# Turning the row maxima of a two-pass attention: DRAM transfer in place of a TensorE transposition

## The reference

```
x = x + cross_attention0(layernorm(x), ctx, mask)     # 6404 keys, padding mask
x = x + self_attention + mixture of experts           # 1024 keys
x = x + (causal self_attention, cross_attention1(x, ctx), feed-forward)
x = x + mixture of experts
# attention, per head:  softmax(q k^T / sqrt(8)) v,   softmax by exp(s - max(s))
```

## Time and profile before

| what | value |
|---|---|
| median of 3 runs | 2885.43 us (2884.71 to 2887.26) |
| the profiled execution's own time | 2884.41 us |
| its span, first to last instruction | 2882.7 us |
| TensorE busy | 2455.8 us, 85% |
| VectorE busy | 2370.1 us, 82% |
| ScalarE busy | 2154.9 us, 75% |
| GpSimd busy | 226.4 us, 8% |
| mean granted TensorE clock | 0.93 of full speed |

### The profile page before, as it was taken

One profiled execution on the slowest core, in us unless ns is written; L12 is line 12 of the kernel. 1 busy time (PEld: TensorE's weight loads), 2 busy tenths in 40 slices (PEclk: granted clock), 3 DMA queues, 4 the chain that ended last, 5 costly groups with the idle time before them and its releaser, 6 DMA issues.

```text
span 2882.7 us, 57521 instructions
## 1 busy us (share of the span) xinstructions
PE 2455.8 (85%) x22475; PEld 777.0 (27%) x22475; DVE 2370.1 (82%) x2782; ACT 2154.9 (75%) x4063; POOL 226.4 (8%) x556
## 2 busy tenths in 40 slices
PE   3499999999999994799459955999999999999955
PEld 2222222222222221222123312222222222222223
DVE  6699999999999983677337635999999999999824
ACT  3189999999999994466315641899999999999941
POOL 4001101010000001000000040000000010000000
PEclk8699999999999997899769966999999999999987
DMA  4211111101101100110111132011101111011000
GB/s 136 71 33 40 41 43 43 41 28 35 34 28 40 29 5 18 49 35 29 36 50 37 39 103 68 26 30 31 38 28 38 31 29 40 28 36 33 6 4 8
DMA packets 76606, 109.17 MB, mean 38 GB/s; under 512 B 17600, under 2 KB 56308, under 8 KB 76340
## 3 DMA queue, kind: packets, MB, share of 16 engines
q1 hardware_dynamic: 74548, 101.12, 12.0%
q0 software_dynamic: 1792, 4.37, 0.8%
HBM read 73.93 MB, written 22.42 MB: 33 GB/s over the span
## 4 chain that ended last, share of the span: by engine, by line
PE 67%; DVE 18%; ACT 6%; issue 4%; SPq 2%; DMA 2%; POOL 1%; ACTq 0%; POOLq 0%; DVEq 0%
PE ps L1280 66%; DVE maxima L1094 12%; ACT probs L884 3%; ACT probs L846 2%; DVE scratch L960 1%; SPq L448 1%; DVE maxima L1053 1%; ACT acc_out L827 1%; POOL probs L648 1%; DMA qa_stage<-q_cross 1%; DMA o_self<-acc_out 0%; PE ps L1288 0%; DVE stats L965 0%; DVE z L975 0%; DVE z L960 0%
## 5 line engine op out<-in xcount | busy, mean ns | idle before, releaser
L1094 DVE TENSOR_REDUCE maxima<-ps 128x1 f32<-128x920 f32 x1792 | 1889.9, 1111 | 102.0 <-PE ps L1280 102.0
L884 ACT ACTIVATE probs<-ps 128x512 f32<-128x512 f32 (+1 forms) x3264 | 1762.4, 594 | 146.3 <-PE ps L1280 146.1
L1280 PE MATMUL ps<-probs,v_stage 128*16 128x256 f32 (+1 forms) x13568 | 1150.0, 403 | 1.5 <-ACT probs L846 1.1
L1280 PE MATMUL ps<-k_stages,qa_stage 64*128 64x460 bf16 (+2 forms) x4032 | 801.5, 370 | 182.9 <-DMA qa_stage<-q_cross 67.3
L1280 PE MATMUL ps<-qb_stage,k_stages 64*128 64x512 bf16 (+4 forms) x3712 | 799.0, 381 | 42.3 <-ACT probs L846 17.6
L1280 PEld LDWEIGHTS ps<-k_stages,qa_stage 64*128 64x128 bf16 (+1 forms) x4032 | 209.5, 94 | 1023.8 <-issue 507.8
L1280 PEld LDWEIGHTS ps<-probs,v_stage 128*16 128x16 f32 x13568 | 234.8, 94 | 422.0 <-issue 364.5
L1053 DVE TENSOR_REDUCE maxima<-ps 128x1 f32<-128x1024 f32 (+7 forms) x256 | 246.8, 987 | 111.6 <-PE ps L1280 110.3
L846 ACT ACTIVATE probs<-ps 128x512 f32<-128x512 f32 (+1 forms) x448 | 229.4, 556 | 141.8 <-PE ps L1280 136.9
L1280 PEld LDWEIGHTS ps<-qb_stage,k_stages 64*128 64x128 bf16 (+1 forms) x3712 | 208.1, 93 | 343.6 <-ACT probs L846 99.9
L654 POOL COPY v_stage<-by_key 128x400 f32<-128x400 f32 (+1 forms) x96 | 40.5, 423 | 1376.0 <-PE ps L1280 1211.4
(11 more groups left out here) (212 smaller groups left out, 932.7 us busy)
## 6 DMA issues: line engine op xcount, KB each, us to landing
k_stages<-k_cross SPq DMA_DIRECT2D x64, 150.2 KB
k_stages<-k_cross SPq DMA_DIRECT2D x64, 150.0 KB
k_cross<-probs SPq DMA_DIRECT2D x24, 384.0 KB, 2.7
scratch<-acc_out SPq DMA_DIRECT2D x512, 16.0 KB
k_stages<-k_cross SPq DMA_DIRECT2D x64, 100.1 KB
k_stages<-k_cross SPq DMA_DIRECT2D x64, 100.0 KB
qa_stage<-q_cross SPq DMA_DIRECT2D x128, 48.0 KB
qb_stage<-q_cross SPq DMA_DIRECT2D x128, 48.0 KB, 4.8
```

The source lines that it names most:

```text
L884: return nc.scalar.activation(probs[0:m, probs_slot(a, j, i), :], ps[0:m, b_bank(a, use), :], ACT.Exp, scale=float(E) ** -0.5)
L1094: nc.vector.tensor_reduce(maxima[:, at, seg:seg + 1], ps[:, A_BANK + 2 * (g % 2):A_BANK + 2 * (g % 2) + 2, 0:a.segment], AX_XY, ALU.max).t ...
L1280: return nc.tensor.matmul(out_, lhsT, rhs, start=start, stop=stop)
```

## The change

In the long attentions the transposition, the copy and the use of the bank ring go. Instead put_maxima, on SyncE, waits for half_parts itself, writes it element by element (128 x 12 elements of 2 bytes) into a DRAM tensor laid out as 12 rows of 128, waits for that to land (`_max_out`), and then issues the two transfers into qb_stage from DRAM. GpSimd waits for `_max_out` before it overwrites half_parts. `ahead` goes from 28 + 12 to 28 + 14 units. Pass B waits for one semaphore fewer in each step.

```
-    a.ahead = len(a.max_units) + 12
+    a.ahead = len(a.max_units) + 14
-    a.turn_step = 20
-    a.turn_tile = a.step_tiles[a.turn_step + 1][0]
...
+                a.m_dram = dram("m_" + a.name, [2, 3, QT, P], BF16)
...
         def tile_use(a, j, i):
-            return 1 + j * (a.key_tiles + 1) + i + (i >= a.turn_tile and j + 1 < a.n)
+            return j * a.key_tiles + i
...
                 def put_maxima(j):
-                    sp.wait_ge(sem(a.name + "_max_rows"), j + 1)
+                    sp.wait_ge(sem(a.name + "_max_parts"), j + 1)
+                    sp.dma_start(a.m_dram[j % 2].rearrange("a t q -> q a t"), half_parts[:],
+                                 allow_slow_non_contiguous=True).then_inc(sem(a.name + "_max_out"), DMA)
+                    sp.wait_ge(sem(a.name + "_max_out"), (j + 1) * DMA)
                     for side in range(a.sides):
                         rows = qb_stage[side * SIDE + ROW_MAX:side * SIDE + ROW_MASK, j % a.ring, 0:BANK]
                         sp.dma_start(rows.rearrange("a (t q) -> a t q", t=QT),
-                                     max_rows[0:3 * QT, :]).then_inc(sem(a.name + "_max_in"), DMA)
+                                     a.m_dram[j % 2]).then_inc(sem(a.name + "_max_in"), DMA)
...
                     if j >= 1:
-                        pool.wait_ge(sem(a.name + "_scores"), turn_use(a, j - 1) + 1)
+                        pool.wait_ge(sem(a.name + "_max_out"), j * DMA)
...
-                        if i == a.turn_tile and j + 1 < a.n:
-                            copy_turned(j + 1)
...
                     free = tile_use(a, j, tiles[-1]) - a.b_banks + 1
                     if free >= 1:
-                        if probs_before(free):
-                            pe.wait_ge(sem(a.name + "_probs"), probs_before(free))
-                        pe.wait_ge(sem(a.name + "_max_rows"), turns_before(free))
+                        pe.wait_ge(sem(a.name + "_probs"), free)
...
-                        if t == a.turn_step and j + 1 < a.n:
-                            turn_maxima(j + 1)
```

More of the change, by code:

```diff
@@ L336, in transformer @@
             a.banks_before = sum(len(b.v_banks) for b in before)
+            if a.cross:
+                a.m_dram = dram("m_" + a.name, [2, 3, QT, P], BF16)
             a.k_dram = dram("k_" + a.name, [3, P, a.keys], BF16)
@@ L378, in tile_use @@
         def tile_use(a, j, i):
-            return 1 + j * (a.key_tiles + 1) + i + (i >= a.turn_tile and j + 1 < a.n)
-        def turn_use(a, j):
-            return 0 if j == 0 else 1 + (j - 1) * (a.key_tiles + 1) + a.turn_tile
+            return j * a.key_tiles + i
         def b_bank(a, use):
@@ L855, in cross_attention @@
             def cross_attention(a):
[L857 to L864, removed]
                 def evacuate(j):
@@ L888, in cross_attention @@
                 done = sem(a.name + "_probs")
-                copy_turned(0)
                 for j in range(a.n):
                     for i in range(a.key_tiles):
-                        if i == a.turn_tile and j + 1 < a.n:
-                            copy_turned(j + 1)
                         if i == a.evacuate_at and j >= 1:
@@ L1440, in pass_a @@
                     last.then_inc(sem(a.name + "_max_scores"), 1)
[L1442 to L1457, removed]
                 def pass_b(j, t):
@@ L1513, in cross_attention @@
                             project_values(a, i, kT, w_v)
-                    if g == n + 4:
-                        pe.wait_ge(sem("values_ready"), a.banks_before + len(a.v_banks))
-                        turn_maxima(0)
+                pe.wait_ge(sem("values_ready"), a.banks_before + len(a.v_banks))
                 given = n_first_a
```

## The result

The changed kernel takes 3298.2 us (median of four runs, 3295.7 to 3306.1), the kernel before 2885.1 on the same chip: a ratio of 1.144 [1.1415, 1.1457]. I had forecast 2859, in a range of 2845 to 2895, so both the direction and the size are wrong. The profiled execution took 3296.7 us.

What follows compares the result with a forecast made beforehand. TensorE and ScalarE were taken to bound the second half of a pass. From 2884.4 us, 30.4 for the transposition came off and 4.1 for `ahead` was added: 2858.1, as a median 2859, range 2845 to 2895.

Steps and rivals of the forecast that it cites:

- The new path, and what it must fit into: Maxima through DRAM before the next pass's step 0: write taken as 6 us, 12.7 us of cover, cost nothing.
- The second half of the same step: At step 0 of pass B: nothing shows up to a 9.2 us write; beyond, each us is paid 62 times.
- The slow-write rival: Step 0 of passes 1 to 31, both attentions: write over 9.6 us cancels the gain, up to 2940; chance 0.22.
- What the turn costs: Transposition in the second half of a pass: removing it gains 0.49 us in each of 62, 30.4 us.
- more gain: Rival: the dropped waits also speed up steps 0 to 5, 0.18 us per pass, 2848 us; chance 0.05.
- What `ahead` adds: Two more pass A units before pass B's first step: 2.06 us per attention, 4.1 us lost.
- The dropped wait: One semaphore wait fewer in each step: could show at step 0, 0 to 11 us gained, taken as 0.
- The change does nothing: Rival: the transposition was hidden, so 2885 us, or 2889 with the two units of `ahead`; chance 0.02.
- half of the gain: Rival: only ScalarE's 0.25 us copy per pass comes back, 15.5 us less 4.1, 2874 us; chance 0.07.

Runs made afterwards that it cites:

- the last run: The VectorE version with `ahead` taken from 28 + 14 back to 28 + 12 units: 2845.9 us, 0.987 of the kernel before.
- the chain of additions: The changed kernel with 56 GpSimd additions behind the split, each waiting for the one before, on a tile of its own: 3322.5 us, measured once.
- the VectorE version: The changed kernel with half_parts transposed in 32x32 blocks on VectorE and eight transfers of 64-byte runs into the query stage, no DRAM write: 2848.7 us, 0.988.

## Why the prediction was wrong

**The step that failed** is "The new path, and what it must fit into". I took 6 us for the write, with 2.7 and 10.5 as bounds; it takes some 15 (14.9 in the median from its issue to the reads'), and the upper bound didn't hold. I had scaled one load of separate elements by their number. The runs showed that number hardly matters (13.9 us for 512, 14.6 for 1536), that the price of 1536 separate elements was well inside my bounds where each has 64 bytes of DRAM to itself (3.6), and that their standing close together makes the rest. That rest comes after the DMA engines have handled the elements, which took 1.9 us. No row of before has a write of that kind, and neither of my bounds came from one; a bound that is scaled from another kind of transfer is not a bound.

**The second half of the same step** was "if that cover falls short, the first products of pass B at step 0 wait", and below 9.2 us "nothing shows". By my own rule 15 us would cost 62 x (15 - 9.2) = 360 us, 3219 in all. The time is 79 us more, and most of the loss is elsewhere: against the same path with a plain write the changed kernel loses 446 us, of which ScalarE's stops in mid-pass are 240 and the waits at step 0 are 55. The other 151 can mostly be found on ScalarE too. Its exponentials' rows in the page (busy time, mean, idle before), the changed kernel first and the plain write second:

```profile
L875 ACT ACTIVATE probs<-ps 128x512 f32<-128x512 f32 (+1 forms) x3264 | 1765.9, 595 | 564.1 <-PE ps L1268 319.4
...
L875 ACT ACTIVATE probs<-ps 128x512 f32<-128x512 f32 (+1 forms) x3264 | 1761.7, 594 | 129.4 <-PE ps L1268 125.2
```

ScalarE is idle 435 us longer, nearly all of the 446. 240 are the stops, and 194 are more waiting for TensorE's products (319.4 against 125.2), the step 0 waits among them. In the restarts TensorE has the lower clock level, and it is busy 144 us longer in all (2574.2 against 2430.4). That it is the clock that lengthens those waits, and not also that the engines are no longer ahead of one another, is argued and not measured by itself. The slow-write rival had the right sign and condition (beyond 9.6 us it decides) at a chance of 0.22. It had the wrong place, and its 2940 was too low.

**What the turn costs** was nearly right: 0.49 us per pass forecast. The plain write shows a pass of 29.5 us where I had 29.6, and a total of 2851.7 against 2883.3 before; with the 4.1 us for the units back that is about 36 us in 62 passes, 0.58 each. It lies between my forecast of 2859 and the 2848 of the "more gain" rival, whose 0.18 us at step 0 may be part of it; no run shows it by itself. One sentence was wrong in passing: VectorE does become the bound without the turn. Its 28 reductions take 29.52 us without a gap, 1.054 each in this part and not 1.028.

**What `ahead` adds**, 4.1 us, agrees with the last run without being proved. **The dropped wait** cannot be told apart from the turn. **The change does nothing** and **half of the gain** are refuted by the plain write.

**The rule that spoke against the change** I had set aside because it has no time for 3 KB. The Trainium skill, "DMA: Bandwidth & Descriptors", section "Rules for kernel authors", calls a plain DMA with a rearranged pattern 19 times slower than the hardware's own transposition; here the rearranged write took some ten times as long as the plain one of the same bytes (about 15 us against 1.4), so the trace agrees with its direction. The size can't be compared, as no run has the hardware's own transposition, and with 64 bytes for each element the rearranged write took 3.6. Its section "Specifications" puts the limit at 512 B, below which an engine reads, modifies and writes. That limit doesn't sort these writes: all are below it, and 24-byte runs landed in 1.4 us, lone elements 64 B apart in 3.6 and side by side in about 15. The runs don't show whether the engine reads and modifies in any of them.

**What stays open** is how the write holds the engines. The semaphore events of the trace pair the products of pass A begun at 666.28 with an increment at 671.91, and those of pass B begun at 666.48 with one at 672.74; VectorE and ScalarE start 0.02 us behind each. So the products had begun over 5 us before their results were released. As the ends of products are modelled, the trace doesn't tell whether they stood still inside TensorE or only their signals came late. Loads of instructions, which the trace has too, start at any point of a pass, without relation to a stop.

The recording of the trace is itself a rival. Each timed execution has a span and a granted clock on record, so I take it that each was traced, and there is no run without. The trace loses events in just these stretches. In the pass with the chain of additions, GpSimd needed some 13 increments between 654.7 and 658.25, and the trace has one. Each write reports its landing by 16 increments. The trace has all 16 for every plain write and every write with its elements apart, but in the median only 10 for those of the changed kernel. So the recording is disturbed by the same writes. Whether it is only disturbed, or whether the engines stand still because their records can't be written, no run tells. The times hold for executions as they were measured here.

## What to carry to other kernels

Count the runs of a small transfer before its bytes, and look at where they land: separate 2-byte elements side by side in DRAM turned a 1.4 us write into one of 15 us and cost 13% of a kernel that didn't use what they wrote. A transfer that is off the critical path is free only if its flight leaves the other engines alone, so test it by itself, as a spare write in the old kernel, before building on it. For turning some rows by 32, VectorE's own transposition took 0.12 us of its stream and needed only 64-byte runs.

## What the runs showed of the hardware

- A write of single 2-byte elements into neighbouring DRAM addresses lands after 14 to 15 us, for 512 elements as for 1536; at 64 and 256 bytes apart after 3.6 and 3.4; as runs of 24 bytes after 1.4. The DMA engines are done with the 1536 packets after 1.9 us (side by side) and 2.2 us (256 bytes apart).
- During such a write TensorE, ScalarE and VectorE stood still together, in 53 of 62 passes of the changed kernel for 1.7 us and more (median 4.6), beginning 5.4 to 11.8 us after its issue. GpSimd, with a chain on a semaphore of its own, stood still later and for less: 72.5 us in a run where ScalarE's stops were 312.6. All of this is seen in traced executions only.
- Single elements read from DRAM 24 bytes apart (2 x 1536) made step 0 wait 23.5 us per pass, and written into SBUF rows (12 x 128) they landed after 11.4 us. Neither stopped an engine in the 11 to 13 us before TensorE waited for them.
- VectorE's transposition of 128x32 bf16 in 32x32 blocks took 0.20 us. The Trainium skill, "VectorE: DVE Perf Modes", section "The three transpose paths", says that it turns each 32x32 block by itself. The kernel of the VectorE version is built on that, with four transfers per half to put the blocks in line.
